# Second attention layer: two score tiles begun with half of the channels, and half of a score tile issued ahead of the transposition of the maxima

## The reference

```python
norm = mean_std_norm(content_feat)
F_Fc = conv1x1(norm, f_w, f_b).reshape(B, C, HW).transpose(0, 2, 1)
G_Fs = conv1x1(norm, g_w, g_b).reshape(B, C, HW)
energy = jnp.einsum('bnc,bcm->bnm', F_Fc, G_Fs)
attention = jax.nn.softmax(energy, axis=-1)
H_Fs = conv1x1(content_feat, h_w, h_b).reshape(B, C, HW)
out = jnp.einsum('bcn,bmn->bcm', H_Fs, attention).reshape(B, C, H, W)
out = conv1x1(out, o_w, o_b)
return out + content_feat
```

## Time and profile before

| | us |
|---|---|
| median of three runs | 2818.74 |
| profiled execution | 2818.41 |
| its span | 2816.7 |
| outside the span | 1.7 |
| PE busy in the span | 2634.8 (94%) |
| DVE busy | 1980.0 (70%) |
| ACT busy | 1286.9 (46%) |
| score tiles' matmuls (L1802), both layers | 136.7 in 512 matmuls |
| maxima of the score tiles (L1295) | 146.2 in 128 reductions |

### The profile page before, as it was taken

One profiled execution on the slowest core, in us unless ns is written; L12 is line 12 of the kernel. 1 busy time (PEld: TensorE's weight loads), 2 busy tenths in 40 slices (PEclk: granted clock), 3 DMA queues, 4 the chain that ended last, 5 costly groups with the idle time before them and its releaser, 6 DMA issues.

```text
span 2816.7 us, 43041 instructions
## 1 busy us (share of the span) xinstructions
PE 2634.8 (94%) x15164; PEld 1832.7 (65%) x15164; DVE 1980.0 (70%) x2249; ACT 1286.9 (46%) x1874; POOL 810.0 (29%) x492
## 2 busy tenths in 40 slices
PE   5899999999999999999999999999999999999894
PEld 4457775577655776567855777557775577656772
DVE  2765777766976768766787677776687666876665
ACT  2463435533365434644346443563336533464434
POOL 0560036400382004800247002650037300481011
PEclk7999999999999999999999999999999999999996
DMA  4300032000410005000050002300032000500016
GB/s 125 74 2 15 12 68 76 17 1 12 107 37 17 1 12 113 31 17 1 30 124 2 17 12 58 86 17 1 12 83 60 17 1 12 112 31 1 1 74 265
DMA packets 46230, 123.39 MB, mean 44 GB/s; under 512 B 9904, under 2 KB 21424, under 8 KB 42416
## 3 DMA queue, kind: packets, MB, share of 16 engines
q1 hardware_dynamic: 46000, 120.36, 16.0%
HBM read 41.96 MB, written 23.86 MB: 23 GB/s over the span
## 4 chain that ended last, share of the span: by engine, by line
PE 71%; issue 9%; DVE 6%; ACT 4%; SPq 4%; POOL 3%; DMA 2%; DVEq 0%; ACTq 0%; POOLq 0%
PE tile L1543 21%; PE pv L1543 11%; PE pv L1667 8%; PE tile L1629 7%; PE tile L1657 6%; PE tile L1802 4%; SPq L582 3%; PE tile L1693 3%; PE pv L1657 2%; PE tile L1824 2%; PE tile L1853 2%; DMA stack<-qk_r 1%; ACT p L854 1%; POOL qk_r L687 1%; PE tile L1721 1%
## 5 line engine op out<-in xcount | busy, mean ns | idle before, releaser
L1123 DVE TENSOR_REDUCE small<-tile 128x1 f32<-128x1024 f32 x512 | 599.9, 1216 | 131.8 <-PE tile L1629 129.4
L854 ACT ACTIVATE p<-tile 128x512 f32<-128x512 f32 (+1 forms) x632 | 405.2, 691 | 220.5 <-PE tile L1657 196.3
L745 POOL TENSOR_TENSOR row_sum<-act 128x256 f32<-128x256 f32 x32 | 41.6, 1317 | 1477.2 <-DVE act L1317 1477.2
L715 POOL TENSOR_TENSOR acc<-acc,p 128x1024 f32<-128x1024 f32 x192 | 450.3, 2380 | 2.7 <-ACT p L854 2.3
L1543 PE MATMUL tile<-qk_r 128*128 128x512 f32 x1536 | 377.9, 395 | 0.0
L1629 PE MATMUL tile<-stack 96*128 96x512 f32 x1024 | 344.7, 435 | 17.2 <-DMA stack<-qk_r 12.1
L1543 PEld LDWEIGHTS tile<-qk_r 128*128 128x128 f32 x1536 | 287.1, 188 | 66.5 <-issue 7.7
L1322 DVE TENSOR_TENSOR pl<-p,ph 128x1024 fp32r<-128x1024 f32 x128 | 158.2, 1236 | 220.8 <-ACT p L936 220.8
L1629 PEld LDWEIGHTS tile<-stack 96*128 96x128 f32 x1024 | 178.5, 192 | 187.0 <-issue 119.4
L1657 PE MATMUL tile<-stack 112*128 112x512 f32 x760 | 269.9, 420 | 24.6 <-ACT p L854 18.0
L1667 PE MATMUL pv<-p,v 128*32 128x512 f32 x2048 | 274.4, 612 | 1.4 <-ACT p L854 1.4
(11 more groups left out here) (285 smaller groups left out, 4459.5 us busy)
## 6 DMA issues: line engine op xcount, KB each, us to landing
stack<-qk_r SPq DMA_DIRECT2D x192, 256.0 KB, 5.0
x_in<-in_x_dram SPq DMA_DIRECT2D x8, 1024.0 KB, 5.0
act<-in_x_dram SPq DMA_DIRECT2D x8, 1024.0 KB, 4.9
x_scratch<-act SPq DMA_DIRECT2D x7, 1024.0 KB, 4.9
z_scratch<-act SPq DMA_DIRECT2D x7, 1024.0 KB, 3.9
stack<-ones SPq DMA_DIRECT2D x16, 256.0 KB, 4.6
w3f<-w3f_scratch SPq DMA_DIRECT2D x8, 512.0 KB, 3.3
fin_rest<-z_scratch SPq DMA_DIRECT2D x3, 1024.0 KB, 9.8
```

What stands on the lines that cost most here:

```text
L715: pe.tensor_tensor(total, first, p0[:, jt % DEPTH, pair, :], ALU.add).then_inc(pool_done, gps.one("add0", *u, jt, pair))
L854: sc.activation(p0[:, jt % DEPTH, pair, first:first + len(heads) * HALF], tile_wait(batch, "st0", *u, jt, k), ACT.Exp, scale=float(D) ** - ...
L1123: ve.tensor_reduce(maxima[:, h, it:it + 1], t, X, ALU.max).then_inc(vector_done, vector.one("max0", g, h, it))
```

## The change

In the section of PE's program where the score tiles are made:

- a score tile's four matmuls now go over the channel tiles outside and the halves inside, in both layers and for all eight tiles (before: halves outside, channel tiles inside);
- a wait for the first channel tile of the keys, `qk_hi(layer, 1, 0)`, stands ahead of the wait for the second one, in both layers;
- in layer 2, the first two score tiles begin between these two waits: each takes its PSUM tile and gets the two matmuls of the first channel tile. After the second wait they get their other two, and the other six tiles follow as before.

Further down, in layer 2, the first half of `scores(0)` (six matmuls, together with the wait for its PSUM tile) moves ahead of `negated`, that is between `v_tile(2, 1)` and the transposition; the wait for `qk_lo(layer, 1, 1)` moves ahead of it in both layers. The second half of `scores(0)` stays behind the transposition.

```diff
+                    def score_parts(it, parts):
+
+                        for kt_ in parts:
+                            for s in halves:
+                                ins = mm(tile[slot("s", layer, it)][:, s], qk_r[:, kt_, 0, 0, it * P:(it + 1) * P],
+                                         qk_r[:, kt_, 1, 0, s], start=kt_ == 0, stop=kt_ == CT - 1)
+                        if CT - 1 in parts:
+                            ins.then_inc(tensor_done, tensor.one("s", layer, it))
+
+                    early = range(2 if layer == 2 else 0)
+                    scalar_wait("qk_hi", layer, 1, 0)
+                    for it in early:
+
+                        free("s", layer, it)
+                        score_parts(it, kts[:1])
                     scalar_wait("qk_hi", layer, 1, 1)
-                    for it in range(NT):
-                        o = free("s", layer, it)
-                        for s in halves:
-                            for kt_ in kts:
-                                ins = mm(o[:, s], qk_r[:, kt_, 0, 0, it * P:(it + 1) * P], qk_r[:, kt_, 1, 0, s],
-                                         start=kt_ == 0, stop=kt_ == CT - 1)
-                        ins.then_inc(tensor_done, tensor.one("s", layer, it))
+                    for it in early:
+                        score_parts(it, kts[1:])
+                    for it in range(len(early), NT):
+                        free("s", layer, it)
+                        score_parts(it, kts)
...
-                    def scores(n):
+                    def scores(n, parts=(0, 1)):
 
                         half, jp = divmod(n, 4)
-                        o = free("st", layer, n)
-                        for q in range(2):
+                        o = free("st", layer, n) if 0 in parts else where("st", layer, n)
+                        for q in parts:
...
                     v_tile(layer, 1)
+                    vector_wait("qk_lo", layer, 1, 1)
+                    if layer == 2:
+                        scores(0, (0,))
                     negated()
-                    vector_wait("qk_lo", layer, 1, 1)
                     for n in range(2):
-                        scores(n)
+                        scores(n, (1,) if (layer, n) == (2, 0) else (0, 1))
                         if n == 0:
                             vector_wait("max_in", layer)
                         less_maxima(n)
```

## The result

The changed kernel takes 2823.36 us (median of 19 runs, 2819.88 to 2826.26), the kernel before, on the same chips, 2817.68 (median of 19, 2806.99 to 2820.48). The ratio is 1.0028, 95% interval [1.0021, 1.0036], that is 5.9 to 10.1 us slower. The medians alone differ by 5.7 and the means, 2823.42 and 2815.45, by 8.0, since the runs of the kernel before spread over 13.5 us. The forecast was 2826.5, 2820.8 to 2830.3, slower by 7.8. The profiled execution of the changed kernel has a span of 2820.7 against 2816.7.

What follows compares the result with a forecast made beforehand. In layer 2, DVE was taken to bound the score tiles and PE everything from `v_tile` on. Layer 2's loss of 6.3 plus 1.5 for the half clock gave 7.8, on 2818.74 a forecast of 2826.5 us, range 2820.8 to 2830.3.

Steps and rivals of the forecast that it cites:

- What bounds the stretch: Layer 2: DVE bounds the score tiles, PE bounds from `v_tile` on; DVE idles 0.67 us for the transposition.
- The early quarter: Layer 2 score tiles: four matmuls move into PE's pause before the second keys wait; gain about 0.11 us per image.
- The six matmuls: Layer 2, half of `scores(0)` ahead of the transposition: transposition 1.38 us later, `scores(1)` 0.89 late per image.
- `max_in`'s wait: Layer 2: the load for `less_maxima(0)` waits 0.2 us for DVE's spreading of `max_in`, in all eight images.
- `v_lo`'s wait: Layer 2: first load of `scores(1)` waits 0.7 to 0.9 us for DVE's low part of the values, all eight images.
- Nothing given back: PE's later pause of 1.30 us moves along with PE's own scores, so all the lost time stays lost.
- the rival of the hidden wait: PE's later pause absorbs the 0.78 us, or `v_lo` doesn't hold `scores(1)`: 2818 to 2821 us; chance 0.17.
- The sum of layer 2: Net loss 0.78 us per image, 0.83 in the last: 6.3 us over eight images, bounds 5.1 to 7.1.
- The half clock: Layer 0: clock falls to 0.50 in some turns, 1.5 us each; one turn more, +1.5, bounds -3.0 to +4.5.
- The reason given: Half clock occurrences lie 337.92 us apart; a longer turn lasts 337.88, so one should more often follow another.
- the 2824.4 at which the prediction let slower begin: Verdict threshold for the whole kernel: 0.2%, 5.6 us, taken as the least difference measurable; slower got chance 0.70.
- The rival of the clock in layer 2: The clock falls in layer 2 as well, 1.5 us per image, 12 us, together 2838; chance 0.04.

Runs made afterwards that it cites:

- experiment 3: Changed kernel with the PSUM tiles of `scores(1)` and `scores(2)` of layer 2 exchanged; measured 1.0003 of the kernel before.
- experiment 7: Changed kernel with `v_tile(2, 1)` moved into PSUM tile `pv`, in quarters behind score tiles, six matmuls still ahead of the transposition; 0.9954 of the kernel before.
- experiment 8: Same as experiment 7, but `scores(0)` whole behind the transposition, as in the kernel before; 0.9989 of the kernel before.
- experiment 4: Changed kernel with all twelve matmuls of `scores(0)`, not six, ahead of the transposition; 1.0052 of the kernel before.

## Why the prediction was right

*What bounds the stretch.* Right, and it is the step on which all hung: DVE bounds the score tiles, PE bounds from `v_tile` on, and the transposition waits for PE. The earlier trace rows had said it in one line, and experiments 3, 7 and 8 show that the sign turns round when that is made otherwise.

*The early quarter.* 0.11 expected, 0.12 measured at the first maximum; nine tenths of a microsecond of PE's work moved, an eighth of that gained, because DVE was only that far from being the bound itself.

*The six matmuls.* The transposition was expected 1.38 later and is 1.40. `max_in`'s wait (0.35 for the loads, where 0.2 was expected) and `v_lo`'s wait (0.83, within the 0.7 to 0.9) are both there, in all eight images. `scores(1)`, measured from `v_tile`'s first load and with the restart in it (3.02 for twelve matmuls instead of 2.88), is 340.09 - 333.00 + 0.14 - (338.63 - 332.34) = 0.94 late; 0.89 was expected. What wasn't in the prediction is which of the two waits can be taken away cheaply; experiment 3 does it with one line.

*Nothing given back.* A turn is 0.81 longer, the local loss of 0.94 less the 0.12. So PE's later pause takes up nothing, and the rival of the hidden wait falls.

*The sum of layer 2.* 6.3 expected, 6.5 by the turns.

*The half clock.* Here the forecast isn't borne out. I took one more turn with it; there are four of seven in both profiles, and as before has one with a longer stretch (338.66), the half clock gives back 1.6 in this pair: the seven turns sum to 4.1 more, where 7 x 0.81 is 5.7. The reason given fits one thing: in the changed kernel the half clock comes at the same place of four turns in a row, in the windows that begin at 1452.40 and 1790.32, 337.92 apart as in the earlier trace rows, and so on to 2466.16. But the first three turns don't have it at all, so that it comes more often by that reason is not shown.

```profile
1452.40:1455.81 3.41, 3.41 (x13) 1.46 (x13) 0.30 (x1) 0.97 (x2) 3.24 (x2) 0.50 0.02 5
1790.32:1793.73 3.41, 3.41 (x13) 1.39 (x13) 0.21 (x1) 1.05 (x3) 3.21 (x3) 0.50 0.02 5
```

The timed difference of 5.9 to 10.1 holds both the 6.5 of layer 2 alone and the 7.8 with the term. The granted clock of the timed runs says no more: it is 0.9803 on average over the changed kernel's 19 runs, and 0.9804, 0.9809 and 0.9807 over the 23, 24 and 11 runs of the kernel before that were taken beside the experiments. One stretch more of 3.41 us at 0.50 would be 0.0006. So these averages leave room for about one more in a run at most, and whether the half clock adds to the loss stays open.

*The number.* The median is 3.1 below the forecast. Of that, 1.1 is the median of the kernel before, which is 2817.68 over 19 runs and was 2818.74 over the three that the forecast was added to; the rest is the 5.7 between the medians where 7.8 was expected. The median also lies below the 2824.4 at which the prediction let slower begin; that the kernel is slower is shown by the interval of the ratio and by the turns. The mechanism and the sum of layer 2 were right. The total doesn't decide on the 1.5: by the medians 6.3 without it is nearer, by the ratio 7.8 with it.

*The rival of the clock in layer 2* falls for this kernel: turns without the stretch in layer 0 are granted 1.00 throughout, with the new pauses in them. It was no empty one, though: with twelve matmuls ahead and the longer pause that follows, it came true in one image of eight (experiment 4).

## What to carry to other kernels

Before work is moved ahead of a short instruction, look in the views by line who waits for that instruction and who is late for it: if the engine that issues it is itself the late one, the work has no pause to fill, and all that hangs on the short instruction moves along. Then follow each reader behind it, down to the buffers that it sets free; here 0.85 of 1.01 us came from a PSUM tile two steps on, and exchanging two tiles took that away. The same move gained once PE's other work was out of the way and that tile no longer held `scores(1)`.

## What the runs showed of the hardware

PE's pause in layer 0 is there in all seven turns of both kernels, 1.40 to 1.55 us long. The granted clock fell to 0.50 at its end or within 0.9 us behind it in four of seven turns, and stayed at 1.00 in the other three, though their pauses are as long; a turn with it was 1.5 us longer, 3.0 where the stretch was twice as long. Five matmuls into that pause kept the clock at 1.00 in all seven turns of the kernel before and took 0.3% off its time, about as much as the change under study cost. As expected, matmuls that go over the halves inside, so that the same stationary operand is loaded twice in a row, issue as before (four in 1.07, as 3 x 0.226 + 0.39).
